# An attention and mixture-of-experts block on one core: side jobs spread over the attention tiles, two head quads in one output bank, four result buffers behind attention

## The reference

```python
# x: 4 x 1024 x 128.  16 heads of 8.
latent = (x @ Wk + x @ Wv) @ W_down_kv
q, k, v = x @ Wq, latent @ W_up_k, latent @ W_up_v
scores = clip(q k^T / sqrt(128)) * exp(-1e-4 * |i - j|)
x = layernorm(x + softmax(clip(scores)) v @ Wo)
logits = x @ w_router                     # 8 experts, the best two of each token
moe = sum over the token's two experts of softmax weight * (silu(x W1a) * (x W1b)) @ W2
x = layernorm(x + moe + (silu(x @ gate_w) * (x @ up_w)) @ down_w)
```

## Time and profile before

| | us |
|---|---|
| median of 3 runs | 778.3 (775.71 to 781.35) |
| the profiled execution | 780.54 |
| its span (first to last instruction) | 778.4 |
| PE busy | 658.6 (85%) |
| ACT busy | 546.6 (70%) |
| DVE busy | 316.5 (41%) |
| POOL busy | 281.0 (36%) |

### The profile page before, as it was taken

One profiled execution on the slowest core, in us unless ns is written; L12 is line 12 of the kernel. 1 busy time (PEld: TensorE's weight loads), 2 busy tenths in 40 slices (PEclk: granted clock), 3 DMA queues, 4 the chain that ended last, 5 costly groups with the idle time before them and its releaser, 6 DMA issues.

```text
span 778.4 us, 12970 instructions
## 1 busy us (share of the span) xinstructions
PE 658.6 (85%) x4815; PEld 296.5 (38%) x4815; DVE 316.5 (41%) x958; ACT 546.6 (70%) x634; POOL 281.0 (36%) x266
## 2 busy tenths in 40 slices
PE   5029899999999999999999998999999869958850
PEld 2013233333333333333333332333333869846530
DVE  1913332444334344433454442432435323236672
ACT  2028798998989899898889986899997224324222
POOL 1900450550333054033205643312101560267772
PEclk9658899999999999999899998999999989979995
DMA  3699564284255228425522855322243686873221
GB/s 114 214 326 395 190 218 174 96 297 176 96 190 187 99 101 311 157 95 190 189 82 96 314 194 195 131 82 96 100 145 119 204 247 195 265 217 101 67 73 49
DMA packets 76915, 132.04 MB, mean 170 GB/s; under 512 B 6512, under 2 KB 51888, under 8 KB 76848
## 3 DMA queue, kind: packets, MB, share of 16 engines
q1 hardware_dynamic: 72736, 123.63, 46.4%
q0 software_dynamic: 3584, 7.35, 3.1%
q10 hardware_dynamic: 528, 0.18, 0.1%
HBM read 82.38 MB, written 50.33 MB: 170 GB/s over the span
## 4 chain that ended last, share of the span: by engine, by line
PE 69%; DVE 11%; ACT 7%; DMA 4%; issue 3%; POOL 2%; another core or an unknown queue 1%; SPq 0%; ACTq 0%; DVEq 0%; POOLq 0%
PE ps L822 26%; PE ps L809 18%; ACT probs L704 7%; PE ps L980 5%; PE ps L764 5%; PE ps L975 4%; DVE ps L1288 3%; PE ps L989 2%; PE ps L844 2%; DMA queries<-stack_dram 2%; PE ps L868 1%; DVE small L1161 1%; DVE osb L1292 1%; PE ps L991 1%
## 5 line engine op out<-in xcount | busy, mean ns | idle before, releaser
L704 ACT ACTIVATE probs<-ps 128x1024 f32<-128x1024 f32 x512 | 482.4, 1038 | 94.2 <-DVE ps L1288 76.6
L822 PE MATMUL ps<-probs,V 128*9 128x512 f32 x2048 | 274.4, 609 | 0.8 <-ACT probs L704 0.5
L809 PE MATMUL ps<-queries,keys 32*128 32x512 f32 (+3 forms) x1408 | 194.5, 418 | 48.4 <-DMA queries<-stack_dram 31.9
L809 PEld LDWEIGHTS ps<-queries,keys 32*128 32x128 f32 x1408 | 95.0, 187 | 209.0 <-ACT probs L704 133.1
L1288 DVE TENSOR_TENSOR ps<-ps,cpk 128x256 f32<-128x256 f32 x256 | 101.8, 428 | 162.4 <-PE ps L809 154.6
L533 POOL TENSOR_TENSOR stage<-qk,rows_sb 128x512 fp32r<-128x512 f32 x28 | 36.8, 1315 | 169.0 <-DVE qk L1149 153.7
L573 POOL DMA_INDIRECT sorted_dram<-xn,slots x56 | 54.9, 980 | 73.2 <-ACT probs L704 35.5
L585 POOL DMA_INDIRECT queries<-result_dram,slots x56 | 57.3, 1023 | 45.4 <-PE ps L994 25.1
L733 ACT ACTIVATE probs<-ps 128x512 f32<-128x512 f32 x42 | 24.8, 599 | 40.4 <-PE ps L980 26.1
L822 PEld LDWEIGHTS ps<-probs,V 128*9 128x9 f32 x2048 | 30.5, 88 | 57.6 <-issue 43.2
L1391 DVE TENSOR_TENSOR probs<-probs,ps 128x512 f32<-128x512 f32 x42 | 28.4, 685 | 56.6 <-PE ps L975 16.3
(11 more groups left out here) (165 smaller groups left out, 586.2 us busy)
## 6 DMA issues: line engine op xcount, KB each, us to landing
stack_dram<-stage SPq DMA_DIRECT2D x64, 512.0 KB, 6.0
keys<-stack_dram SPq DMA_DIRECT2D x32, 1024.0 KB
queries<-stack_dram SPq DMA_DIRECT2D x32, 512.0 KB
keys<-expert_dram SPq DMA_DIRECT2D x36, 192.0 KB
sorted_dram<-y_pre SPq DMA_DIRECT2D x1, 4608.0 KB, 20.6
result_dram<-probs SPq DMA_DIRECT2D x18, 256.0 KB
rows_sb<-expert_dram SPq DMA_DIRECT2D x20, 192.0 KB
V<-expert_dram SPq DMA_DIRECT2D x16, 192.0 KB
```

The costliest lines, as they stand in the source:

```text
L704: nc.scalar.activation(probs[:, m % 3, 2 * j:2 * j + 2, :], ps[:, 2 * s:2 * s + 2, :], ACT.Exp, scale=SCALE).then_inc(exp_done, 1)
L809: last = mm(bank[2 * s + i][:, lo:hi], keys[rows, u, kt // CT, v, tok(kt % CT)], queries[rows, u, v, lo:hi], start=True, stop=True)
L822: last = mm(bank[OUT_BANK][32 * i:32 * i + HD + 1, :], V[:, c // 2 % 2, kt, 4 * (Q % QUADS) + i, :], probs[:, m % 3, i, :], start=(kt == 0 ...
```

## The change

1. **Side jobs.** `side_places` is written anew: three tables (last chunk, odd, even). Jobs have one to four parts of whole 128-column tiles or of columns, and the jobs stand wider apart. The statistics behind `wo` are cut: DVE's bn_stats stay with the job, the aggregation comes two tiles after the job's last part. Routing steps hang on the distance from `lg`.
2. **Two quads in one bank.** V holds for each pair of heads 27 columns: 8 of V and a one, 9 zeros, 8 of V and a one. `outputs` takes 18 columns of them: value and zero columns in a pair's first quad, zero and value columns in its second, and both are summed in the same 18 rows over 16 tiles. Quads are taken in the order 0, 2, 1, 3. So there are 16 evacuations instead of 32, and 16 `o` jobs, each of two quads. The copy of V and the division by the sums are two instructions instead of one.
3. **Counts.** DVE adds up the one-hot rows over a chunk's four tiles itself (`running`), and the `cnt` job is 2 matmuls of 8 columns instead of 5 of 40 to 8.
4. **Behind attention.** Four result buffers `y_blk` and four fetch buffers `gathered` instead of two each; shared expert 2 stands behind unit 9 instead of before unit 8 and shared 3 and 4 later too; the sums (`COMBINE_AFTER`) are placed anew; POOL makes the last chunk's normalised rows after 14 of the last 24 scatters instead of after all, its scatters wait for a point of the ring one place earlier, `x` and `lg` of the last chunk stand one work item earlier, and the second norm's power comes two chunks behind its fetch instead of one.

```diff
-        V = sb("V", [P, 2, NT, HEADS, HD + 1])
+        V = sb("V", [P, 2, NT, HEADS // 2, 3 * (HD + 1)])
...
-        gathered = queries[:, :, :, :].bitcast(F32)
+        gathered = [queries[:, n, :, :].bitcast(F32) for n in range(2)] + [osb[:, :, :], x_res[:, :, :]]
...
-        y_blk = pflat[:, 2 * HALF:4 * HALF].rearrange("p (u s) -> p u s", u=2)
+        y_blk = [pflat[:, 2 * HALF:3 * HALF], pflat[:, 3 * HALF:4 * HALF], pflat[:, 11 * HALF:12 * HALF], a_tok[:, 0, :]]
+        YD, GD = len(y_blk), len(gathered)
...
             d, p = c - 1, c + 2
-            z = 0 if c % 2 else 4
-            places = {("xT", p): (0 if c % 2 else 2,), ("o", 4 * d + 3): (z + (1 if c % 2 else 0),),
-                      ("q", p): (z + 2, z + 3) if c % 2 else (z + 1, z + 2), ("a", d): (6 if c % 2 else 7,),
-                      ("k", p): (z + 8, z + 9), ("wo", d): (z + 10, z + 11), ("o", 4 * c): (z + 13,),
-                      ("x", d): (z + 16,), ("norm", p): (z + 17,), ("lg", d): (z + 18, z + 19), ("o", 4 * c + 1): (z + 21,),
-                      ("cnt", d): (z + 24,), ("v", p): (z + 25, z + 26), ("o", 4 * c + 2): (z + 27,)}
+            if c == NCH - 1:
+                places = {("o", 2 * d + 1): (1,), ("a", d): (4,), ("wo", d): (7, 8), ("x", d): (14,), ("lg", d): (16, 17),
+                          ("o", 2 * c): (18, 19), ("cnt", d): (22,)}
+            elif c % 2:
+                places = {("xT", p): (0,), ("o", 2 * d + 1): (1,), ("q", p): (4, 5, 6), ("a", d): (7, 8), ("k", p): (9,),
+                          ("wo", d): (13, 14), ("v", p): (15, 16), ("o", 2 * c): (19, 20), ("x", d): (22,),
+                          ("lg", d): (23, 24), ("norm", p): (26, 27), ("cnt", d): (29,)}
+            else:
+                places = {("o", 2 * d + 1): (1, 2), ("xT", p): (3, 4), ("q", p): (5,), ("a", d): (7, 8), ("k", p): (10, 11),
+                          ("wo", d): (12, 13), ("v", p): (16, 17, 18, 19), ("o", 2 * c): (20, 21), ("x", d): (23, 24),
+                          ("lg", d): (26,), ("norm", p): (27, 28), ("cnt", d): (30,)}
             if c == 0:
-                places.update({("norm", 0): (14,), ("norm", 1): (15,)})
+                places.update({("norm", 0): (13,), ("norm", 1): (14,)})
             if c == NCH - 2:
-                places["flag", 0] = (12,)
-            gone = [n for n in places if n[0] in ("xT", "q", "k", "v") and p >= NCH or n[0] == "norm" and n[1] >= NCH
+                places["flag", 0] = (14,)
...
         LAST = NCH - 1
-        shared_before = {0: 0, 4: 1, 8: 2, 12: 3, 15: 4}
...
-        LAST_STEPS = {0: "o", 1: "a", 2: "wo", 7: "x", 9: "lg"}
-        COMBINE_AFTER = {17: [0], 20: [1], 23: [2], 25: [3], 30: [4], len(work): [5, 6]}
+        LAST_STEPS = {0: "o", 1: "a", 2: "wo", 6: "x", 8: "lg"}
+        COMBINE_AFTER = {16: [0], 19: [1], 21: [2], 24: [3], 28: [4], 32: [5], len(work): [6]}
         FINISH_ORDER = list(range(NCH))
-        ROWS_AT = [21, 24, 26, 31] + [len(work)] * 4
+        ROWS_AT = [22, 25, 27, 31] + [len(work)] * 4
...
-                if c >= 2:
-                    pool.wait_ge(combined, c - 1)
+                if c >= GD:
+                    pool.wait_ge(combined, c - GD + 1)
...
             pool.wait_ge(slots_ready, 3)
-            for k in range(GROUPS[0][1] * CT, GROUP * CT):
-                send(k, ring_ready, 3 * (k - GROUPS[0][1] * CT))
-            ln1_rows(LAST)
+            first = GROUPS[0][1] * CT
+            for k in range(first, GROUP * CT):
+                send(k, ring_ready, 3 * (k - first - 1))
+                if k == first + 6:
+                    ln1_rows(LAST)
...
+            units_stored(FIRST_UNITS)
+            for c in range(GROUP):
                 if c == GROUPS[1][0]:
-                    for u in range(2):
-                        pool.wait_ge(results_stored[u], 16 * UNITS // 2)
+                    units_stored(UNITS)
                 fetch(c)
-                ln2_power(c - 1)
-            ln2_power(GROUP - 1)
-            ln2_power(LAST)
+                if c >= 2:
+                    ln2_power(c - 2)
+            for c in range(GROUP - 2, NCH):
+                ln2_power(c)
...
-                    if u >= 2:
-                        act.wait_ge(results_stored[u % 2], 16 * (u // 2))
-                    nc.scalar.activation(y_blk[:, u % 2, :], ring_bank(name), ACT.Copy).then_inc(ring_by_act, 1)
+                    if u >= YD:
+                        act.wait_ge(results_stored[u % YD], 16 * (u // YD))
+                    nc.scalar.activation(y_blk[u % YD], ring_bank(name), ACT.Copy).then_inc(ring_by_act, 1)
...
+                half, k = Q % 2, quad(Q) % 2 * 4
...
-                if kt == 0 and Q:
-                    pe.wait_ge(o_evacuated, Q)
+                if kt == 0 and half == 0 and Q:
+                    pe.wait_ge(o_evacuated, Q // 2)
                 pe.wait_ge(exp_done, 2 * m + 2)
                 for i in range(4):
-                    last = mm(bank[OUT_BANK][32 * i:32 * i + HD + 1, :], V[:, c // 2 % 2, kt, 4 * (Q % QUADS) + i, :],
-                              probs[:, m % 3, i, :], start=(kt == 0), stop=(kt == NT - 1))
+                    last = mm(bank[OUT_BANK][32 * i:32 * i + 2 * (HD + 1), :],
+                              V[:, c // 2 % 2, kt, k + i, half * (HD + 1):(half + 2) * (HD + 1)], probs[:, m % 3, i, :],
+                              start=(kt == 0 and half == 0), stop=(kt == NT - 1 and half == 1))
                 last.then_inc(pv_done, 1)
...
                     elif what == "cnt":
-                        count_chosen(k)
+
+                        pe.wait_ge(chosen_ready, k + 1)
+                        mm(dst[:, 0:E], before, running[:, CT, :], start=True, stop=True)
+                        last = mm(dst[:, E:2 * E], all_ones, running[:, CT, :], start=True, stop=True)
...
             def choose(d):
-                tt(chosen[:, 0:CT, :], onehot[:, 0, d, :, :], onehot[:, 1, d, :, :], ALU.add).then_inc(chosen_ready, 1)
+
+                link(tt(running[:, 1:CT + 1, :], onehot[:, 0, d, :, :], onehot[:, 1, d, :, :], ALU.add))
+                for t in range(2, CT):
+                    link(tt(running[:, t, :], running[:, t, :], running[:, t - 1, :], ALU.add))
+                tt(running[:, CT, :], running[:, CT, :], running[:, CT - 1, :], ALU.add).then_inc(chosen_ready, 1)
...
 
-            def evacuate(Q):
-                dve.wait_ge(pv_done, NT * (Q + 1))
-                copy(osb[:, Q % 2, :], bank[OUT_BANK]).then_inc(o_evacuated, 1)
+            def evacuate(R):
+                dve.wait_ge(pv_done, 2 * NT * (R + 1))
+                copy(osb[:, R % 2, :], bank[OUT_BANK]).then_inc(o_evacuated, 1)
...
                         dve.wait_ge(side_kept, numbers[name])
-                        statistics(y_pre[:, :], stats, mv, var, var_ready)
+                        for i in range(CT):
+                            rest(nc.vector.bn_stats(stats[:, i, :], y_pre[:, tok(i)]))
...
+                    since = {name[0]: m - TPC * cc - at_tiles[-1] for name, at_tiles in side_places(cc).items() if name[1] == d}
+                    if since["wo"] == 2:
+                        dve.wait_ge(dve_chain, links[0])
+                        aggregate(stats, mv, var, var_ready)
+                    if since["lg"] == 2:
+                        route_lanes(d)
+                    if since["lg"] == 3 and d < GROUP:
                         choose(d)
...
+                    if since["lg"] == 5:
+                        dve.wait_ge(gexp_ready, d + 1)
+                        route_weights(d)
...
-                if m and m % NT == 0:
-                    evacuate(m // NT - 1)
+                if m and m % (2 * NT) == 0:
+                    evacuate(m // (2 * NT) - 1)
```

190 lines of the change are left out of this document (85 added, 105 removed).

## The result

The kernel after takes 751.8 us (median of 4 runs, 750.70 to 753.72), the one before 778.7 (4 runs, 775.71 to 781.35): 0.966 of the time, 95% interval 0.963 to 0.969. The forecast was 746 us, range 728 to 764. The profiled execution took 750.7 us, with a span of 748.6.

A forecast was written before the change was run, and what follows sets the result against it. ACT's exponentials and their stops bound attention, 70% of the time; POOL's fetches, begun after SP's stores, set the end. 780.5 less 27 (attention) and 5.5 (behind it) gives 748, 746 us at the median; range 728 to 764.

The forecast's parts named there:

- Large stops: ACT's six largest stops in chunks 2 and 3 all go: 7.3 us per two chunks, 22 us over chunks 1 to 6.
- rival B: Attention: the 14 other stops of each chunk pair halve too, 13 us more, 733 us in all; chance 0.17.
- Less PE work against wider operands: PE in attention: 14.5 us saved on transpositions and counts cancels 18 us for loading 18 columns; 0 net.
- Rival C: Output matmuls: 18-column loads cost more than in proportion; slower from 72 ns more per load, 836 us at 100; chance 0.03.
- First and last chunk: Attention's chunk 7 gains 1.5 us from half its evacuations, chunk 0 gains 1 us from a later xT; 2.5 together.
- The clock: Chunk 4's dip to granted clock 0.95, which made it 2.56 us longer than chunk 2, goes: 2.6 us.
- Behind attention: From attention's end to the execution's end: 5.5 us shorter, between 0 and 12.
- SP's delay: Stores of units 4 and 5: PE's 5.34 us wait for the last chunk's rows goes, saving 9.87 less 5.39, 4.5 us.
- the first sum: Sum on DVE behind attention: same distance to unit 9 in the list, so DVE and PE wait about as before; 0.
- Four buffers: Result and fetch buffers behind attention: they remove waits of ACT and POOL, but POOL's fetches had next to none; 0.
- rival D: Behind attention nothing is gained, PE's own end takes the place of POOL's: 752 us or some more; chance 0.11.
- A (stops move): Attention: stops move to other tiles, so it gives only a third, 9 us; 764 us in all; chance 0.17.

The follow-up runs named there:

- whole_turns: Kernel after with side jobs o, a, xT, x, q and v in one tile each (two for v) instead of parts over several tiles; 757.6 us, 0.9727.
- one_quad_per_bank: Kernel after with one quad per output bank again: nine stationary columns, an evacuation and an o job for every quad; 755.9 us, 0.9730.
- stats_at_once: Kernel after with the residual's statistics finished at once in the tile of wo, instead of aggregating two tiles later; 749.5 us, 0.9632.
- tail_only: Kernel before with its old attention, but everything behind attention as in the kernel after; first chip, 769.5 us, 1.0041.
- sums_later: Kernel after with the first three sums two steps later in the list; 730.0 us, 0.9535 on the first chip; 747.0 us, 0.9599 on the third.
- attention_only: Kernel after with its new attention, but everything behind attention as in the kernel before; first chip, 732.2 us, 0.9548.
- list_of_before: Kernel after with only the work list behind attention as before; buffers, early rows, scatters and powers stay new; first chip, 736.3 us, 0.9615.

## Why the prediction was right, point by point

**Large stops, forecast 22 us: right, and too small.** The six named stops are gone, and the 14 others of the pair shrank from 7.1 to 4.1 us as well, which was rival B's mechanism (B had them halved). Chunks 1 to 4 give 5.0, 4.8, 5.4 and 7.4 us, the last with the clock's 2.6 in it. Of the causes that I named, parts are worth some 5 us (whole_turns) and two quads in one bank some 6 (one_quad_per_bank). The split of the statistics, which stood among the reasons on DVE, is worth nothing with the new places (stats_at_once). That the places carry the rest, and so most, is by difference; no run puts them or the longer `cnt` back.

**Less PE work against wider operands, forecast 0: off in both of its terms, and not separated in the time.** PE was busy for 492.7 us of attention against 513.6 before, 21 us less, and on the first chip 19 less (510.9 in tail_only, 491.7 in sums_later), where my terms had 3.5 more. Nine more columns cost a tile 0.01 us, so 2 to 3 us of PE time for the kernel instead of my 18. The single load grew by about what I took, 9 ns: its mean record is 88 ns with 9 columns and 96 with 18, and 104 with 27, over 1000 loads and more each. But hardly any of it shows on PE. The Trainium skill, "TensorE: Matmul & The Clock Gate", section "LDWEIGHTS (loading the stationary operand)", gives columns divided by 1.2 in ns, 7.5 for nine more: the trace's 8 agrees with that as a difference, though not the whole record, 88 ns for 9 columns. The warning that I took from its section "Part 3: Packing small matmuls — row/col tiling", that such loads overlap only where row groups differ, is not borne out here: all heads use all rows, and no more than 0.01 us of the eight times 8 ns shows on PE. Rival C's price of 72 ns is far off.

**First and last chunk, forecast 2.5 us:** they gave 4.2 and 2.4, 6.6 in all, too small a term (chunk 0 alone is from 64.9 to 67.1 us in three profiles of the kernel after). **The clock, forecast 2.6:** the dip of chunk 4 is gone, as forecast; it belonged to the old attention, since tail_only on the first chip has it as well (69.16 us at 0.95). But I took the dip alone and did not see that the kernel before has a long stop too, in chunk 6, at granted clock 0.95, the same chunk that the chip without stops runs in 64.57 us under the same code (tail_only):

```profile
462.66:533.22 70.56, 60.18 (x65) 0.95 0.41 142
```

```profile
464.53:529.10 64.57, 59.86 (x66) 1.00 0.45 155
```

It costs 6.0 us there. In the kernel after it stands in chunk 5 and costs 71.58 less 64.24 in that chunk and 62.61 less 60.50 in the next, 9.5 us. Without any such stop, attention goes from 537.95 to 500.71 us, 37 less (tail_only against sums_later, whole attention in one window):

```profile
54.75:592.70 537.95, 482.26 (x512) 0.98 0.48 169
```

```profile
53.38:554.09 500.71, 479.25 (x512) 0.98 0.52 182
```

So on a chip with stops the gain is 33.4, and the forecast of 27 was low by 10 us, of which the stops hide nearly 4.

**Behind attention, forecast -5.5, measured +4.1 (here) and +2 to +3 (tail_only): wrong.** Three steps failed.
- "with it SP's delay, 9.87 less 5.39, 4.5 us": PE's wait is gone, but the first fetch came only 1.3 us earlier (1.4 on the first chip). Stores 4 and 5 gained 3.3 of the 4.5; but the stores of units 0 to 4 take 25.7 us where they took 23.8, since the one gap of 9.30, the stop near 600, is 3.9 us over SP's pace. On the first chip, which has no such gap, the start still gains only 1.4, because the wait does not cost SP its full length everywhere: in attention_only it is still there, 4.15 us long, and SP's stores around it (591.47 and 598.37) are 6.90 apart, 1.5 over its pace:

```profile
591.87 0.63 PE L778 MATMUL ps<-cpk,xn 128*128 128x128 f32 x4 [4.15 <-POOL xn L566]
```

- "I count 0" for the first sum: this is the step that mattered most. DVE waits 6.5 us longer (3.1 on the first chip, 14.91 against 11.79). Some half of the 6.5, 3.5, is that it reaches the sum 0.8 us after the first fetch begins (655.46 less 14.91, against 639.78) where it was 4.3 before; the rest is that the first eight fetches take 3.0 us longer to be used. In the new list shared expert 2 no longer stands ahead of unit 8, where it gave PE and DVE work while SP stored; I take this for the reason, and no run moves it alone. PE fills its banks and stops, POOL's fetches wait for PE's place in the ring, and the row of fetches takes 3.2 us more. sums_later takes the stop away and shortens the row, by 3.2 us on the first chip and 1.5 on the third.
- "Four buffers ... so 0", and that the end hangs on POOL alone: the last sum starts 4.8 us after the last fetch, where it was 2.6, because DVE takes PE's last result at 730.81 first. Before, that sum waited for the rows of the last fetch:

```profile
761.25 2.31 DVE L1439 SCALAR_TENSOR_TENSOR qk<-queries,small,qk 128x128 f32<-128x128 f32 x8 [2.96 <-DMA queries<-result_dram,slots]
```

  PE's end had become as late as POOL's, which is rival D's mechanism. list_of_before shows that the rest of the tail's change costs on its own; which part of it was not separated.

**The rivals.** A (stops move) and C are refuted, B is right for attention, D for the tail. That the total fell near the forecast is luck: B's surplus and D's loss are of one size. The 752 us of rival D came even nearer, with an attention term of 27 us that was too small as well.

## What to carry to other kernels

Spread a job over the tiles in which the pacing engine has slack, and space the jobs; here the new attention gave all of the gain, most of it by difference through the places, and the stops nobody had named shrank with the named ones. When work is moved in a list, recompute for every blocking wait how far ahead of its data the engine now arrives; "the same distance in the list" is not the same distance in time. A forecast whose total is right can rest on two errors: read each stretch by itself, and compare the stretches on one chip.
